# Gate biases by a ScalarE copy and one-hots by VectorE in a graph-network kernel

## The reference

```python
def _gru_cell(x, h, wih, whh, bih, bhh):
    gi = x @ wih.T + bih
    gh = h @ whh.T + bhh
    ir, iz, inn = jnp.split(gi, 3, axis=-1)
    hr, hz, hn = jnp.split(gh, 3, axis=-1)
    r = jax.nn.sigmoid(ir + hr)
    z = jax.nn.sigmoid(iz + hz)
    n = jnp.tanh(inn + r * hn)
    return (1.0 - z) * n + z * h
...
w_e = (eh @ en2_w.T + en2_b).reshape(-1, D, D)
for _ in range(STEPS):                       # 6
    msg = jnp.einsum('ei,eio->eo', out[src], w_e)
    agg = jax.ops.segment_sum(msg, dst, num_segments=n_nodes) + conv_bias
    m = jax.nn.relu(agg)
    h = _gru_cell(m, h, gru_wih, gru_whh, gru_bih, gru_bhh)
    out = h
```

## Time and profile before

| | |
|---|---|
| median of 3 runs | 38341.23 us |
| the runs | 38295.71, 38341.59, 38341.23 us |
| profiled execution | 38293.46 us |
| its span | 38291.7 us |
| start of the first of the six steps, in the span | 15484.9 us |
| length of a step | 3796 us |
| of it the main loop / the tail / the update with its borders | 3634 / 59 / 103 us |

### The profile page before, as it was taken

One profiled execution on the slowest core, in us unless ns is written; L12 is line 12 of the kernel. 1 busy time (PEld: TensorE's weight loads), 2 busy tenths in 40 slices (PEclk: granted clock), 3 DMA queues, 4 the chain that ended last, 5 costly groups with the idle time before them and its releaser, 6 DMA issues. The chain is left out here.

```text
span 38291.7 us, 454886 instructions
## 1 busy us (share of the span) xinstructions
PE 27942.1 (73%) x97246; PEld 17043.7 (45%) x97247; DVE 27081.4 (71%) x45800; ACT 11786.0 (31%) x26941; POOL 29657.2 (77%) x30158
## 2 busy tenths in 40 slices
PE   5333346655653333899989998999899989999998
PEld 5333334455653333444444444444444444444444
DVE  7443432222531111899989999999999899989998
ACT  0000011111200000344444444444444444444444
POOL 1776777677247677799879988998899789979997
PEclk8555556655655555999999999999999999999999
DMA  0220012311311011111111111111111111111111
GB/s 19 47 48 26 23 51 82 69 28 28 89 26 14 14 14 14 43 46 47 42 45 45 46 41 46 46 47 39 47 46 47 39 47 47 47 40 46 47 47 39
DMA packets 1452380, 1590.44 MB, mean 42 GB/s; under 512 B 953756, under 2 KB 1115535, under 8 KB 1346959
## 3 DMA queue, kind: packets, MB, share of 16 engines
q1 hardware_dynamic: 743720, 1056.16, 8.7%
q0 software_dynamic: 645120, 473.02, 7.6%
q10 hardware_dynamic: 63360, 59.50, 0.5%
HBM read 1342.34 MB, written 246.33 MB: 41 GB/s over the span
## 5 line engine op out<-in xcount | busy, mean ns | idle before, releaser
L1999 PE MATMUL l3m_p_w<-en,l3m_hid 128*128 128x512 f32 x39936 | 19494.9, 615 | 1244.1 <-DVE l3m_prod L2079 1134.0
L2057 DVE TENSOR_REDUCE l3m_xg<-l3m_prod 128x32 f32<-128x1024 f32 x9984 | 12022.8, 1204 | 0.0
L1918 POOL DMA_INDIRECT l3m_xg<-wide_table,l3m_mt x9984 | 9776.2, 979 | 2639.5 <-issue 1506.2
L1927 POOL TENSOR_TENSOR l3m_prod<-l3m_rest,l3m_xg 128x384 f32<-128x384 f32 x9984 | 10093.2, 1011 | 282.4 <-ACT l3m_rest L1973 105.3
L1999 PEld LDWEIGHTS l3m_p_w<-en,l3m_hid 128*128 128x128 f32 x39936 | 6834.4, 191 | 6393.3 <-issue 4867.2
L1973 ACT COPY l3m_rest<-l3m_p_w 128x384 f32<-128x384 f32 x9984 | 4772.1, 478 | 11362.0 <-PE l3m_p_w L1999 11358.1
L2075 DVE TENSOR_TENSOR l3m_prod<-l3m_p_w,l3m_xg 128x512 f32<-128x512 f32 x9984 | 6752.9, 676 | 153.6 <-DMA l3m_xg<-wide_table,l3m_mt 134.1
L2015 PEld LDWEIGHTS l3m_p_sum<-room,l3m_apart 128*125 128x125 f32 x21120 | 3942.5, 197 | 5633.5 <-issue 5633.5
L1961 ACT ACTIVATE l3m_apart<-iota_lo,l3m_lo 128x125 f32<-128x125 f32 x10560 | 4195.1, 401 | 0.0
L2015 PE MATMUL l3m_p_sum<-room,l3m_apart 128*125 x21120 | 3332.5, 246 | 687.2 <-issue 607.0
L872 POOL DMA_INDIRECT l2a_rows<-table,l2a_mt x1664 | 1586.7, 954 | 1637.0 <-DMA l2a_mt<-dst_meta 1130.1
(11 more groups left out here) (368 smaller groups left out, 21007.8 us busy)
## 6 DMA issues: line engine op xcount, KB each, us to landing
l3m_hid<-hid_t SPq DMA_DIRECT2D x624, 1024.0 KB, 5.2
l3m_xg<-wide_table,l3m_mt POOLq DMA_INDIRECT x9984
hid_t<-l_hid SPq DMA_DIRECT2D x110, 1024.0 KB, 4.0
order_src_bk<-dst_bucket SPq DMA_DIRECT2D x52, 808.0 KB
order_dst_bk<-src_bucket SPq DMA_DIRECT2D x52, 808.0 KB
l_rec<-by_dst SPq DMA_DIRECT2D x110, 272.0 KB
l_xg<-table,l_mt POOLq DMA_INDIRECT x1760
l1a_xg<-table,l1a_mt POOLq DMA_INDIRECT x1760, 2.4
```

The lines of the kernel that those rows point to most:

```text
L1918: pool.indirect_dma_start(xg[s][:, j, 0:2 * D], None, wide_table[:, :], bass.IndirectOffsetOnAxis(ap=mt[s][:, j, 0:1].bitcast(I32), axis=0 ...
L1927: pool.tensor_tensor(o_i(prod[j % RING][:, OWN:HD]), o_i(rest[j % RING][:, :]), state_of(s, j, REST), ALU.mult).then_inc(pooled, 1)
L1999: ins = pe.matmul(p_w[j % 2][:, c * 512:(c + 1) * 512], hid[s][:, j * P:(j + 1) * P], en2[:, c * 512:(c + 1) * 512], start=True, stop=True)
L2057: dve.tensor_reduce(xg[s][:, j, 2 * D:3 * D], o_i(prod[j % RING][:, :]), AX, ALU.add).then_inc(msgs, 1)
```

## The change

Three edits:

1. **Gate biases.** Once, in a new phase `l3b` ahead of the steps, TensorE spreads the biases over 125 partitions (the old product, done once) and VectorE copies them into `gates` (125 x 512, SBUF). In each turn of the update the product L2147 is gone; instead ScalarE copies `gates` into the bank `p_g` (new function `base`): turns 0 and 1 at the very start, turn n after the tanh of turn n-2. TensorE waits for that copy (semaphore `based`) before the first product with `whh`, where it had waited for VectorE's second operation (`n_in`).
2. **Narrower input product.** The product with `wih` goes over 384 columns in place of 512.
3. **One-hots of the tail.** For groups 104 to 109 VectorE makes them with `find`: 16 comparisons (128 x 125, `is_equal`) for each group in place of ScalarE's 16 Abs and 4 Relu. `find` for group g + 2 stands ahead of `add` for group g; each quarter waits until TensorE has used up that quarter of the same buffer. ScalarE keeps the clearing. In the tail TensorE waits for `found`, not `hits`.

`PLACE` goes from 97 to 89, and the main loop of VectorE begins at the same instruction number as before.

```diff
-PLACE = 97
+PLACE = 89
...
+        gates = sb("gates", [LO, 4 * P])
+        with Phase("l3b") as ph:
+            p_b = ph.ps("p_b", [P, 4 * P])
...
+                    pe.matmul(p_b[0:LO, :], ones[0:2, 0:LO], gbias[:, :], start=True, stop=True).then_inc(spread, 1)
...
+                    dve.wait_ge(spread, 1)
+                    dve.tensor_copy(gates[:, :], p_b[0:LO, :])
...
                         with act.Fori(TG // 2, PG // 2) as i:
                             for s in range(2):
                                 clear(i * 2 + s, s)
-                                for j in range(G):
-                                    distance(i, s, j)
...
-                                pe.wait_ge(hits, g * 4 + 4)
+                                pe.wait_ge(found if tail else hits, g * 4 + 4)
...
+                        def find(i, s):
+                            g = i * 2 + s
+                            dve.wait_ge(lo_in[s], i * 16 + 16)
+                            for j in range(G):
+                                if j % 4 == 0:
+                                    dve.wait_ge(summed, g * G + (j + 4))
+                                ins = dve.tensor_scalar(apart[s][:, j, :], iota_lo[:, :], lo[s][:, j:j + 1], None, ALU.is_equal)
+                                if j % 4 == 3:
+                                    ins.then_inc(found, 1)
...
-                        with dve.Fori(TG // 2 - 1, PG // 2) as i:
+                        with dve.Fori(TG // 2 - 1, PG // 2 - 1) as i:
                             for s in range(2):
+                                find(i + 1, s)
                                 dve.load([add_regs[0]], off_d[0:1, bass.ds((i * 2 + s) * G, 1)])
                                 add(i * 2 + s, s)
+                        for s in range(2):
+                            dve.load([add_regs[0]], off_d[0:1, (PG - 2 + s) * G:(PG - 2 + s) * G + 1])
+                            add(PG - 2 + s, s)
...
-                                if q >= 2:
-
-                                    pe.wait_ge(n_in, q - 1)
+                                pe.wait_ge(based, q + 1)
                                 to = p_g[q % 2][0:LO, :]
-                                pe.matmul(to, ones[0:2, 0:LO], gbias[:, :], start=True, stop=False)
...
-                                pe.matmul(to, m_t[q % 2][:, :], wih[:, :], start=False, stop=True).then_inc(g_ok, 1)
+                                pe.matmul(to[:, 0:3 * P], m_t[q % 2][:, :], wih[:, 0:3 * P], start=False, stop=True,
+                                          skip_group_check=True).then_inc(g_ok, 1)
...
+                        def base(q):
+                            act.copy(p_g[q % 2][0:LO, :], gates[:, :]).then_inc(based, 1)
+
+                        base(0)
+                        base(1)
...
                                 act.activation(new[q % 2][:, :, :], new[q % 2][:, :, :], ACT.Tanh).then_inc(n_ok, 1)
+                                if n < Q:
+                                    base(n)
```

More of the change, by code:

```diff
@@ L1766, in _ @@
                                   by_group[:, :, 0:1].broadcast_to([1, PG, G]), ALU.subtract)
+        gates = sb("gates", [LO, 4 * P])
+        with Phase("l3b") as ph:
+            p_b = ph.ps("p_b", [P, 4 * P])
+            spread = ph.sem("spread")
+            with nc.Block() as block:
+                @block.tensor
+                def _(pe):
+                    pe.matmul(p_b[0:LO, :], ones[0:2, 0:LO], gbias[:, :], start=True, stop=True).then_inc(spread, 1)
+                @block.vector
+                def _(dve):
+                    dve.wait_ge(spread, 1)
+                    dve.tensor_copy(gates[:, :], p_b[0:LO, :])
+            ph.end()
         class StateProducts:
@@ L1855, in build @@
                 rows_in = [ph.sem(f"rows_in{s}") for s in range(2)]
-                distances, hits, mats, used, copied, pooled, msgs, joined, summed, added, cleared, begun = (ph.sem(n) for n in (
+                distances, hits, mats, used, copied, pooled, msgs, joined, summed, added, cleared, begun, found = (ph.sem(n) for n in (
                     "distances", "hits", "mats", "used", "copied", "pooled", "msgs", "joined", "summed", "added",
-                    "cleared", "begun"))
+                    "cleared", "begun", "found"))
                 LATE, LATER = 2, 6
@@ L2094, in _ @@
                         dve.drain().then_inc(used, USED)
+                        dve.sem_inc(found, TG * 4)
                         dve.sem_inc(msgs, MSGS)
@@ L2120, in build @@
                 p_g = [ph.ps(f"p_g{s}", [P, 512]) for s in range(2)]
-                t_ok, m_ok, g_ok, s_ok, n_in, n_ok, h_ok = (ph.sem(n) for n in (
-                    "t_ok", "m_ok", "g_ok", "s_ok", "n_in", "n_ok", "h_ok"))
+                t_ok, m_ok, g_ok, s_ok, n_in, n_ok, h_ok, based = (ph.sem(n) for n in (
+                    "t_ok", "m_ok", "g_ok", "s_ok", "n_in", "n_ok", "h_ok", "based"))
                 def part(q, k):
```

## The result

| | before | changed |
|---|---|---|
| median of 6 runs | 38341.41 us | 38200.13 us |
| the runs lie between | 38295.71 and 38349.11 us | 38197.63 and 38205.38 us |
| profiled execution | 38293.46 us | 38200.28 us |
| its span | 38291.7 us | 38198.5 us |

The changed kernel is faster: ratio 0.9964, 95% interval 0.9954 to 0.9975, or 141 us. The forecast was 38180 us, in a range from 38110 to 38290.

What follows compares the result with a forecast made beforehand. VectorE bounds the untouched main loop, ScalarE the tail, TensorE's products the update. Tail -56, update -88 and +6 elsewhere gave -138 us: 38155 or 38203 by the runs' two places, middle 38180, range 38110 to 38290.

Steps and rivals of the forecast that it cites:

- The total: Whole kernel: tail -56, update -88, one-time and reset costs +6, in all -138 us, bounds -109 to -155.
- The tail: Tail groups fall from 8.18 to 6.8 us on TensorE: 9.4 us a step, 56 in all, bounds 49 to 58.
- The allowance of 0.05 us per gap: Tail: idle time allowed between TensorE's groups, lowering the gain from 9.7 to 9.4 us a step.
- The precedent: Another stage's same 32-column products: 478 passes in 100 us without a gap, 0.209 us each, at half clock.
- the cover: Tail: a whole TensorE group of 6.8 us in which VectorE's comparisons, add and clearing were to be hidden.
- The ring: Update turn: gate, tanh, bias copy, products, next gate set the pace at 2.71 us, 0.48 less than today.
- The update's start: First gates at 3.65 and 6.6 us at half clock, third at 9.3, last at 68.9 us after the first product.
- Once: Phase `l3b` costs 5 us (3 to 10), two more semaphores to reset 1 to 2; together 6 us.
- The clock falls: Rival, update: TensorE's idling loses full clock, ring stays at 4.06 us, total +48 us against before; 6%.
- The tail bound by VectorE: Rival, tail: comparisons or a delayed add keep groups at 8 us, only the update's -82 us is won; 7%.
- Slower by fetch: Rival, main loop: moved code needs an instruction fetch in each of 51 turns, +168 us net; 4%.
- Nothing in the update: Rival, update: something unseen (state wait, stores) bounds it, only the tail's -50 us is won; 5%.

Runs made afterwards that it cites:

- e6_copy_twice: Changed kernel with a second equal ScalarE copy, into an unused bank, ahead of each bias copy from turn 2 on: 40380.54 us (one run), turns 3.23 us.
- e5_early: Changed kernel with the bias copy moved ahead of the gate of the turn before, behind the relu of `m_t`: 40224.21 us, ratio to before 0.9943.
- e1_before_again: The kernel before, unchanged, traced a second time, on another chip: 40471.09 us, main loops 3639.5 to 3640.8 us.
- e9_two_rows: Changed kernel with the old two-row bias product put back for each update's first three turns, into an unread bank: 40438.75 us (one run).
- e7_place97: Changed kernel with `PLACE` 97 instead of 89, VectorE's code eight instructions later: 40422.12 us (one run), 146 us less than before on the same chip.

## Why the prediction was right, point by point

**The total.** 138 us were forecast, 141, 151 and 149 measured, in the three comparisons of like with like. By the parts it is 150: 61 for the tails and 93 for the gates, less 4 paid elsewhere, so both large terms were some 5 us too small, and that 141 lies so near to 138 is in part luck. The runs of both medians fell at the upper place. There the sum gives 38203, and 38200 came; the middle between the places (38180), which I took, is 20 us off. The first pair of profiles, of unlike places, would have spoken for 93 only.

**The tail.** Forecast 9.4 us a step, measured 58.92 - 48.74 = 10.2: 61 in all, not 56, and over the bound of 58. The allowance of 0.05 us per gap was not needed, there is none; and a group takes 6.72 us, not 6.8. The precedent had 0.209 us per pass, and 0.210 is what came. VectorE's share was oversized: I added the comparisons by their duration of 0.28 us, and 16 of them took 3.20 us, 0.2 each, since neighbours overlap. It changed nothing, as the cover was 6.8 us wide; nor did the wait for `lo`, which the forecast did not have. The registers' loads and the clearing stayed hidden, as costed.

**The ring.** 2.71 forecast, 2.72 measured, and its members one by one: 0.48 and 0.49 to the copy, 0.58 and 0.59 for it, 0.05 and 0.05 to TensorE, 1.60 and 1.59 to the gate. `e6_copy_twice` and `e5_early` show that the copy was on the path, which the forecast had only argued.

**The update's start.** First gate at 3.65, measured 3.58. The second was set at half clock (6.6 us); since the clock rose at 3.8 to 6.2 it came 0.2 to 1.4 us sooner. So the last gates are at 67.7 to 68.9 us, not at 68.9 throughout, and the update gave 93 us for 88. The term that was mis-sized is the clock's rise: I had put a gain in it at nothing, and allowed only for a later one. Nor is the other side of the difference fixed: the same old kernel took 502.0 us for this part in one execution and 494.1 in another (`e1_before_again`), so the 93 could as well have been 85.

**Once.** Phase `l3b` was put at 5 us. In the changed kernel's trace the time from the first product of `l3i` to that of `l3s` is 22.7 us, before 19.8: 2.9. The border by the last add is 3.92 us, before 3.79: 0.8 for six steps, 1 forecast. The main loops of the lower place, 5 us longer in all, are not explained by anything here.

**The rivals.** *The clock falls:* no. PEclk stays 1.00 from its rise to the last gate in every update of the changed kernel, with TensorE idle for a quarter of the time, also in `e6_copy_twice` with 1.23 us of idling ahead of each turn's products. The one fall on record is that in `e9_two_rows`. The Trainium skill, "TensorE: Matmul & The Clock Gate", section "A second HAM failure mode: psum-queue depth-cycling", would have it swing here; no trace of the changed kernel shows that. *The tail bound by VectorE:* no, VectorE waits for TensorE (mostly 0.81 us for a quarter). *Slower by fetch:* no; there are 145 + 33 transfers where there were 146 + 34, and `e7_place97` shows that for VectorE a place eight instructions off is as good. The Trainium skill, "Advanced Engine Details and Errata", section "ISA Cache", gives two lines of 256 instructions. VectorE's main loop has some 226 in a turn in the trace, so by that rule it fits at either place, and the runs agree. *Nothing in the update:* no, it gave the larger part.

**What the forecast left on the table.** It saw that the ring gives back 0.48 us of 1.27. The same sum says what a copy outside of the ring is worth, 0.6 us a turn, and `e5_early` took it: 2.14 on the mean.

## What to carry to other kernels

Work taken off the engine that is the limit is worth only what the next ring leaves of it; add the ring up member by member from rows, from one start to the next of the same instruction, and where the moved work stands in it, look for a place one turn earlier. When two traces of the same code differ in a part that nobody touched, run the old kernel again before explaining it, and compare executions of the same place. Where an engine is full, a precedent from another stage of the same trace (here 32-column products without a gap) tells how full it can get.

## What the runs showed of the hardware

- One program's executions lie at two places, some 40 us apart here: joins of 903 to 909 ns against 920 to 923, gathers of 979 against 982 ns on average, main loops of 3634 against 3640 us.
- The same kernel took 5.5 to 5.8% longer on two other chips, nearly all of it ahead of the six steps. In the two stages of L518, which make up 616 of 2149 us, GpSimd's gathers are as long as elsewhere, but stand further apart; the cause is open. The page's row of one of them (busy, mean, idle before), of before in `e1_before_again`, where the first chip's has 1629.7, 979 and 604.6:

```profile
L518 POOL DMA_INDIRECT by_dst<-order_src_rec,order_src_idx x1664 | 1620.3, 974 | 920.3 <-issue 490.9
```

- TensorE ran its 32-column products for 47 us, busy all the time, at half clock (0.50) from end to end.
- The granted clock rises 3.0 to 17.5 us after an update's first product, having been at half through the tail. Rises later than 6.4 us occurred only with the product over two rows in the stream.
- A copy of 125 x 512 in float32 from SBUF to PSUM takes ScalarE 0.59 us, and its neighbour starts after 0.52.
